# Expert selection row built by scalar_tensor_tensor with a tile of zeros instead of tensor_scalar

## The reference

```python
x = x + tanh(g_xattn[0]) * xattn(layernorm(x), ctx_2048, ...)
```

```python
scores = sqrt(softplus(xt @ gate_w.T))
_, idx = top_k(scores + gate_b, 2)
w = scores at idx, divided by their sum
pos = place of this token in its expert's buffer (cumulative count)
buf = zeros((E, CAP, D)).at[e, pos].add(x_pairs)
h = silu(buf @ W1.T) * (buf @ W3.T)          # per expert, 256 -> 176
out = h @ W2.T                               # per expert, 176 -> 256
y = sum over the token's two experts of w * out[e, pos]
x = x + tanh(g_ffn[0]) * (y + shared)
```

## Time and profile before

| | |
|---|---|
| median of 3 runs | 402.17 us (401.6 to 403.28) |
| the profiled execution | 401.21 us, span 399.5 us |
| TensorE busy | 351.5 us (88%) |
| VectorE busy | 307.4 us (77%), 656 instructions |
| ScalarE busy | 250.4 us (63%) |
| GpSimd busy | 124.7 us (31%), 117 instructions |
| granted TensorE clock, mean | 0.951 of full speed |

### The profile page before, as it was taken

How to read it: one execution, slowest core, us unless ns; L and a number is a source line. 1 busy time by engine, 2 the same in 40 slices (tenths; PEclk the granted TensorE clock), 3 DMA queues, 4 the chain that set the end, 5 groups by cost and what they waited for, 6 DMA issues and landing times.

```text
span 399.5 us, 14020 instructions
## 1 busy us (share of the span) xinstructions
PE 351.5 (88%) x5793; PEld 271.5 (68%) x5793; DVE 307.4 (77%) x656; ACT 250.4 (63%) x412; POOL 124.7 (31%) x117
## 2 busy tenths in 40 slices
PE   0896859999999999998999999989846789999993
PEld 0672539778777777866866967876635577888872
DVE  3988796877686787686777677769895968999983
ACT  3575637687677687776777766676712626676761
POOL 6151552024123132232213200010101254787770
PEclk9999889999999999999999999999975858999999
DMA  7979963276295187177346117752000009534001
GB/s 248 206 169 209 236 150 90 79 131 165 77 155 161 54 146 193 55 114 184 93 74 125 42 38 122 184 156 71 3 2 2 1 19 330 164 116 159 2 0 48
DMA packets 34513, 45.67 MB, mean 114 GB/s; under 512 B 3995, under 2 KB 30299, under 8 KB 34323
## 3 DMA queue, kind: packets, MB, share of 16 engines
q1 hardware_dynamic: 33395, 43.74, 45.2%
q0 software_dynamic: 640, 0.78, 1.0%
q10 hardware_dynamic: 416, 0.26, 0.3%
HBM read 25.08 MB, written 0.47 MB: 64 GB/s over the span
## 4 chain that ended last, share of the span: by engine, by line
PE 79%; DVE 11%; issue 4%; ACT 3%; DMA 2%; DVEq 0%; SPq 0%; ACTq 0%
PE PS L1035 38%; PE PS L1100 10%; PE PS L1078 9%; PE PS L1111 8%; PE PS L1362 4%; PE PS L1321 4%; PE PS L1345 2%; DVE mtop L798 2%; DMA PT_all<-L_xattn_wkv 2%; DVE mx L794 1%; DVE cT L715 1%; PE PS L1088 1%; PE PS L1278 1%; DVE KN L743 1%; PE PS L1311 1%
## 5 line engine op out<-in xcount | busy, mean ns | idle before, releaser
L794 DVE TENSOR_REDUCE mx<-PS 112x1 f32<-112x500 f32 (+1 forms) x128 | 114.3, 934 | 45.4 <-PE PS L1078 45.3
L1035 PE MATMUL PS<-cT,wkvT 128*128 128x500 f16 x288 | 71.7, 389 | 20.2 <-DVE cT L715 13.6
L501 ACT ACTIVATE PT_all<-PS 128x1344 f32<-128x1344 f32 x64 | 82.5, 1289 | 9.4 <-PE PS L1100 9.2
L1035 PE MATMUL PS<-wkvT,cT 128*125 128x256 f16 x576 | 70.6, 275 | 0.0
L1035 PEld LDWEIGHTS PS<-wkvT,cT 128*125 128x125 f16 x576 | 64.5, 138 | 5.3 <-issue 0.7
L395 POOL TENSOR_TENSOR cT<-c_in,cT 128x1000 f16<-128x1000 f32 x18 | 37.4, 2080 | 85.9 <-ACT cT L479 85.9
L1035 PEld LDWEIGHTS PS<-cT,wkvT 128*128 128x128 f16 x288 | 27.9, 99 | 53.1 <-issue 11.6
L486 ACT ACTIVATE KN<-PS,col_in 128x500 f16<-128x500 f32 x48 | 32.5, 677 | 41.1 <-PE PS L1035 41.1
L1078 PE MATMUL PS<-arena,QC 96*112 96x500 f16 x192 | 51.6, 376 | 2.4 <-issue 2.2
L1100 PE MATMUL PS<-QC,arena 98*128 98x112 f16 x768 | 48.6, 213 | 3.0 <-ACT QC L521 3.0
L1100 PEld LDWEIGHTS PS<-QC,arena 98*128 98x128 f16 x768 | 41.0, 98 | 9.0 <-ACT QC L521 4.5
(11 more groups left out here) (208 smaller groups left out, 453.4 us busy)
## 6 DMA issues: line engine op xcount, KB each, us to landing
arena<-KN SPq DMA_DIRECT2D x144, 125.0 KB, 3.9
c_in<-ctx SPq DMA_DIRECT2D x24, 500.0 KB, 5.1
cT<-W SPq DMA_DIRECT2D x11, 352.0 KB
c_in<-W SPq DMA_DIRECT2D x6, 352.0 KB
cT<-W SPq DMA_DIRECT2D x11, 176.0 KB
arena<-place_far SPq DMA_DIRECT2D x1, 1568.0 KB, 9.1
c_in<-W SPq DMA_DIRECT2D x6, 176.0 KB
PT_all<-L_xattn_wkv SPq DMA_DIRECT2D x1, 512.0 KB, 6.3
```

The source lines that it names most:

```text
L501: act.activation(PT_all[:, u % 4, :].rearrange("p (c k) -> p c k", c=CH), PS[:, 3:6, 0:4 * TP], ACT.Exp, scale=SCORE).then_inc(s["exp_done ...
L794: dve.tensor_reduce(mx[:, u % 2, k:k + 1], PS[0:TP, k:1 + k * (CH - 1), 0:CW], AX.XY, ALU.max).then_inc(s["red_done"], 1)
L1035: ins = mm(out_, w(a, h), x_(b, h), start=first and k == 0, stop=last and k == len(todo) - 1)
```

## The change

`turned_select(e)` compares with another instruction: (place_row == slot_of) + zeros, with the tile of zeros as a second tensor input. The tile of zeros is allocated on 128 partitions in place of 112, so that its first 448 columns can be that input for all 128 slots. Values and everything else stay as they are.

```diff
-        zero16 = sb("zero16", [TP, 512], F16)
+        zero16 = sb("zero16", [128, 512], F16)
...
                 need(dve, "added", e - 1)
-                dve.tensor_scalar(selT[e % 2], place_row[:, e, :], slot_of[:, 0:1], None, ALU.is_equal).then_inc(s["st_done"], 1)
+                dve.scalar_tensor_tensor(selT[e % 2], place_row[:, e, :], slot_of[:, 0:1], zero16[0:CAP, 0:T],
+                                         ALU.is_equal, ALU.add).then_inc(s["st_done"], 1)
```

## The result

| | before | changed |
|---|---|---|
| median | 401.19 us (12 runs, 396.31 to 404.27) | 403.34 us (12 runs, 400.96 to 404.19) |
| the profiled execution | 401.21 us, span 399.5 | 402.05 us, span 400.3 |
| period of the expert loop in the profile | 3.946 us | 4.119 us |

The changed kernel is slower: ratio 1.0069 [1.0039, 1.0099], so about 2.8 us on 402, with an interval from 1.6 to 4.0. The forecast was 4.55 us more, a median of 406.7 us. The two profiles differ by less, 0.84 us, because the stages ahead of the loop, which the change leaves alone, happened to be 1.17 us shorter in the second: line 974 first runs at 332.41 in place of 333.58. From its first to its last run, 15 experts on, it takes 59.59 us against 57.56, 2.03 us more.

The account below looks back on a forecast made before the run. VectorE was taken to set the expert loop's period, TensorE following with at most 0.17 us of room. 13 x 0.35 = 4.55 us gave 405.8 us on the profiled execution, 406.7 on the median; range 403.3 to 408.3.

Parts of the forecast that it names:

- The sign: Whole kernel slower, chance 0.78, against faster 0.12 and same 0.10.
- the place: Step from line 974 to VectorE's next instruction in the expert loop grows from 1.07 to 1.42 us.
- two elements at a time: New line 974 runs two elements a cycle but waits for 449: 1.5 us more, 403.7 us; chance 0.06.
- closed loop: Expert loop: 963, then 449, then 974 hold one resource; period is seven other VectorE steps plus one run of 449.
- the second rival: New line 974 doesn't wait for GpSimd; its step falls from 1.07 to 0.54 us, time to 400.2 us; chance 0.12.
- the speed of the new form: Line 974 alone, 448 elements: 0.62 us at the slow end, which was taken; 0.39 at two elements at a time.
- the three covered runs: Line 974's first and last two runs sit before other waits; at most 0.05 us of the first comes through.
- the 13 runs: Runs of line 974 behind line 449, said to stay so; each 0.35 us longer, 4.55 us in all.
- the step that failed: Expert loop: 963 stays 0.21 us ahead, so 449 takes the resource at 963's end, before the new 974 asks.
- the order it assumed: 963, then 449, then 974, with 974 ending 0.47 to 0.49 us after 449's end.
- what 446 would do: GpSimd's 446 starts reading some 0.4 us later, ends about 348.0, still 0.8 us before the next 449.

Follow-up runs that it names:

- All four versions that open the loop: Changed kernel with zeros in PSUM (3.807 us) or 446 cut (3.812); kernel before with 974 ahead of 963 (3.807) or 449 cut (3.806).
- the PSUM version: Changed kernel with line 974's zeros read from a free PSUM bank instead of SBUF; period 3.807 us, ratio to before 0.9942 [0.9898, 0.9986].
- The copy behind 981: Changed kernel plus a VectorE copy of 384 elements from PSUM between 981 and 974; period 4.242 us, ratio to before 1.0099 [1.0052, 1.0145].
- the versions with 974 ahead of 963: turned_select moved ahead of select: on the changed kernel period 3.988 us, ratio to before 1.0027; on the kernel before 3.807 us, 0.9941.
- the tiny copies: Changed kernel plus a one-element VectorE copy from PSUM, so two short instructions stand between 963 and 974; period 4.184 us, one run, 406.12 us.

## Why the prediction was right or wrong

The sign, the range and the place were right; the mechanism inside was wrong. That the kernel got slower at all came by a path that the forecast did not have, so sign and range are in part luck: the median of 403.34 us lies at the very end of the range, which went down to 403.3 for a case that did not occur (two elements at a time). By the ratio it would be 402.17 x 1.0069 = 404.9 us.

Right: VectorE and GpSimd share a closed loop through a resource that they hold in turns, and TensorE had about 0.14 us of room per expert. All four versions that open the loop end at 3.81 us; the second rival put the gain at 2.0 us (400.0 to 400.7) and the PSUM version, which is that rival built, has 0.9942, 2.3 us. Right too: the speed of the new form, 0.67 us alone where 0.62 was estimated at one element at a time and 0.39 at two; and next to nothing from the three covered runs: the first step of the loop is 3.48 us in place of 3.58, and from the last of the 13 runs (384.51, now 385.31) to the end of the span it is 14.99 us in both profiles.

Wrong, the step that failed: "449 still takes the resource when 963 ends, before the new instruction asks". The new instruction goes first, by its form. It never waits, which was the second rival's condition; that rival's gain of 2.0 us didn't come, since it left out that GpSimd now waits for line 974. Line 974 fell from 1.15 to 0.67 us where 1.50 was forecast. What it costs comes back elsewhere: 449 ends 1.02 us after 974, 446 moves to just ahead of 859, and holds it for 0.32 us. The cost per expert is 4.119 - 3.946 = 0.173 us where 0.35 was forecast, 2.0 to 2.3 us over the loop where 4.55 was. The copy behind 981 shows that the forecast's own numbers were sound for the order it assumed: there 974 ends 0.48 us behind 449, as forecast (0.48), and 446 takes 1.74 us where about 1.9 was forecast.

The rows could not tell this. In the earlier trace rows GpSimd's line 458 was already reading when line 932 came, and in the earlier trace rows the instruction that waited was of the old form; no row had an instruction with both inputs in SBUF come up at the end of another with GpSimd waiting.

The working did ask what 446 would do: "starts reading some 0.4 us later ... and still has 0.8 us until the next 449". It looked only at GpSimd's next instruction. It did not ask what stood on VectorE at that time with both inputs in SBUF, and that was 859.

The Trainium skill ("SBUF — State Buffer", Who interferes with whom) was right that two SBUF inputs contend with GpSimd's reads, and the measurement agrees twice: 859 is held 0.32 us by 446, and with one input of 974 in PSUM 449 no longer waits for 974 (1.46 us in place of 2.46). The same section says that issue order decides who blocks, and not the shape of the operation. The old form agrees (449 at 344.52, 974 at 345.05, 449 first). The new one doesn't (449 at 343.36, 974 at 344.13, 974 first; in the second expert 449 at 335.40, 974 at 335.89), and the measurement decides.

## What to carry to other kernels

When VectorE and GpSimd work side by side, list the VectorE instructions that have both inputs in SBUF, and those of a form like the f16 tensor_scalar here, whose 0.32 us became 1.15 beside GpSimd. Then add up their and GpSimd's turns around the loop: that sum can set the period while the chain of waits shows almost only TensorE. One input in PSUM, or an order in which the short tensor_scalar is through before GpSimd's turn, took the line out of the loop; the slower form only changed who waits. When an instruction no longer waits, look at which one is now late, and at what it meets there.

## What the hardware showed unexpectedly

A waiting GpSimd instruction (449) is passed over by a VectorE instruction with both inputs in SBUF when that starts within 0.13 us of the end of another such one, and not when it starts 0.39 us after it. This is seen only where GpSimd was waiting at that end: in the earlier trace rows line 446 begins at 319.70, 0.01 us after the end of line 932, and line 933, 0.04 us after that end, is held (0.65 us, against an estimate of 0.22). A VectorE tensor_scalar on f16 (0.32 us alone) is not let past even with no gap at all.

GpSimd's tensor_scalar of 1.49 us holds a VectorE instruction with both inputs in SBUF only in its first part. Line 859, started 0.15 us behind it, ends as if it had begun 0.48 us after 446's start and then run its usual 0.88 us; the last 1.0 us of 446 adds nothing to it. The same sum fits the versions with 974 ahead of 963 and with the tiny copies, where 859 ends 1.35 and 1.36 us after 446's start.
